# Where a recurrent kernel starts its indirect DMAs inside a step, and where it seeds its PSUM banks

## The reference, cut to what matters

```python
xW = jnp.einsum('ntd,dh->nth', x, Wx) + b          # x: 2 x 1024 x 256

def step(prev_h, xw_t):
    next_h = jnp.tanh(xw_t + prev_h @ Wh)          # Wh: 256 x 256
    return next_h, next_h
_, hs = jax.lax.scan(step, h0, jnp.swapaxes(xW, 0, 1))   # 1024 steps, one after the other

logits = x_flat @ gate_w.T                         # x_flat: the 2048 states, 8 experts
top_v, top_i = jax.lax.top_k(logits, 2)
combine = ...                                      # softmax of the two, by expert and token
hidden = silu(x_flat @ wg[e].T) * (x_flat @ wu[e].T)     # per expert, 256 -> 1024
acc = acc + combine[e][:, None] * (hidden @ wd[e].T)     # 1024 -> 256
return x + acc
```

## Time and profile before

| | us |
|---|---|
| median of 3 runs | 847.75 (846.58 to 849.95) |
| the profiled execution | 847.57 |
| its span in the profile | 845.5 |
| PE busy / ACT busy / DVE busy / POOL busy | 741.6 / 479.4 / 441.4 / 112.0 |
| the tanh (L843), 1024 of them: busy; idle before them, for PE's L474 | 161.9; 300.4 |
| the ring's low part (L1175), 1024: busy; idle before them, for ACT's L843 | 166.1; 339.3 |
| matmuls of the ring (L474, wh_hi): idle before them, for DVE's L1175 | 74.0 |

### The profile page before, as it was taken

One profiled execution on the slowest core, in us unless ns is written; L12 is line 12 of the kernel. 1 busy time (PEld: TensorE's weight loads), 2 busy tenths in 40 slices (PEclk: granted clock), 3 DMA queues, 4 the chain that ended last, 5 costly groups with the idle time before them and its releaser, 6 DMA issues.

```text
span 845.5 us, 41906 instructions
## 1 busy us (share of the span) xinstructions
PE 741.6 (88%) x17106; PEld 645.1 (76%) x17106; DVE 441.4 (52%) x2572; ACT 479.4 (57%) x2839; POOL 112.0 (13%) x104
## 2 busy tenths in 40 slices
PE   6555555699999999999999999999999999998894
PEld 4443444588888888888888888888888888887784
DVE  4776767454454545454544445454545444455542
ACT  4776777555555555555655556555555555554442
POOL 1000000001111101101020111111021101123222
PEclk7555555599999999999999999999999999999997
DMA  4676766501111111111120111111111111111111
GB/s 131 194 198 183 205 186 184 183 10 38 19 35 22 35 22 24 34 20 31 22 41 16 29 23 34 29 26 25 19 39 22 34 16 29 24 17 39 29 29 23
DMA packets 35149, 49.01 MB, mean 58 GB/s; under 512 B 5232, under 2 KB 21616, under 8 KB 34928
## 3 DMA queue, kind: packets, MB, share of 16 engines
q1 hardware_dynamic: 27200, 36.53, 15.7%
q0 software_dynamic: 7488, 9.57, 7.2%
q10 hardware_dynamic: 272, 0.26, 0.1%
HBM read 35.57 MB, written 12.88 MB: 57 GB/s over the span
## 4 chain that ended last, share of the span: by engine, by line
PE 78%; DVE 6%; ACT 6%; DMA 4%; issue 4%; another core or an unknown queue 0%; POOLq 0%; ACTq 0%; SPq 0%; DVEq 0%
PE bank L474 35%; PE bank L597 24%; PE bank L619 12%; DVE state L1175 4%; ACT bank L843 4%; DMA arena<-w_all 3%; PE bank L628 3%; PE bank L456 1%; PE bank L576 1%; DMA out<-y_sb,place_now 1%; PE bank L568 1%; ACT w_hi L829 1%; DVE arena L1103 0%; DMA b_sb<-bias_in 0%
## 5 line engine op out<-in xcount | busy, mean ns | idle before, releaser
L1175 DVE TENSOR_TENSOR state<-bank,state 128x4 f16<-128x4 f32 x1024 | 166.1, 162 | 353.7 <-ACT bank L843 339.3
L474 PE MATMUL bank<-state,wh_hi 128*128 128x4 f16 (+1 forms) x4204 | 264.8, 168 | 83.1 <-DVE state L1175 74.0
L843 ACT ACTIVATE bank<-bank 128x4 f32<-128x4 f32 x1024 | 161.9, 158 | 306.1 <-PE bank L474 300.4
L474 PEld LDWEIGHTS bank<-state,wh_hi 128*128 128x128 f16 x4204 | 176.5, 98 | 172.4 <-DVE state L1175 115.3
L474 PE MATMUL bank<-state,wh_lo 128*128 128x2 f16 x4096 | 245.4, 163 | 0.0
L474 PEld LDWEIGHTS bank<-state,wh_lo 128*128 128x128 f16 x4096 | 177.5, 97 | 0.0
L835 ACT ACTIVATE state<-bank 128x4 f16<-128x4 f32 x1024 | 175.1, 171 | 2.8 <-PE bank L474 2.7
L597 PE MATMUL bank<-x_T,w_hi 128*128 128x128 f16 (+1 forms) x1856 | 154.8, 206 | 4.6 <-issue 2.6
L619 PE MATMUL bank<-arena,w_hi 128*128 128x128 f16 (+1 forms) x1600 | 140.1, 208 | 0.3 <-DVE arena L1110 0.2
L597 PE MATMUL bank<-x_T,w_lo 128*128 128x128 f16 (+1 forms) x928 | 138.1, 206 | 0.0
L597 PE MATMUL bank<-arena,w_hi 128*128 128x128 f16 (+1 forms) x1344 | 129.0, 211 | 1.7 <-issue 1.3
(11 more groups left out here) (141 smaller groups left out, 971.4 us busy)
## 6 DMA issues: line engine op xcount, KB each, us to landing
arena<-w_all SPq DMA_DIRECT2D x96, 256.0 KB
xrow<-expert_rows SPq DMA_DIRECT2D x82, 66.0 KB
early<-xT SPq DMA_DIRECT2D x17, 128.0 KB
expert_rows<-pad SPq DMA_DIRECT2D x8, 132.0 KB, 3.2
expert_rows<-rows,slot POOLq DMA_INDIRECT x34
out<-y_sb,place_wide POOLq DMA_INDIRECT x30
out<-y_sb,place_now POOLq DMA_INDIRECT x20, 3.2
arena<-wh_in ACTq DMA_DIRECT2D x1, 256.0 KB, 4.2
```

The costliest lines, as they stand in the source:

```text
L474: return pe.matmul(out, w[:, k, m * P:(m + 1) * P], moving, start=False, stop=False, skip_group_check=True)
L843: act.activation(h32_at(n), preact(n), ACT.Tanh, scale=1 / SCALE).then_inc(s_h32, 1)
L1175: v.tensor_tensor(lo[:, i, :, B * tt:B * tt + B], h32_at(n).rearrange("p (c b) -> p c b", c=2), hi[:, i, :, B * tt:B * tt + B], ALU.subtra ...
```

## The change

Every indirect DMA of the loop is pinned in one way: a scatter or an add at step n waits for the tanh of step n-1. The adds move from o = 16 to 18, the scatters from o = 0, 6, 12 to 0, 4, 10, all steps that have one of VectorE's long operations. The seeds move from the steps 0, 1, 2 of a block to 3, 4, 5 (the first block keeps its place), and the waits for them move along.

```diff
+SEED_AT = 3
-ADD_AT, SCATTER_AT = (16, 22), (0, 6, 12)
+ADD_AT, SCATTER_AT = (18, 22), (0, 4, 10)
...
     def count_step(blk):
-        return scatter_steps(blk)[0] - 1 if blk == NBLK - 1 else scatter_steps(blk)[1] - 3
+        return scatter_steps(blk)[0] - 1 if blk == NBLK - 1 else scatter_steps(blk)[1] - 2
...
+        def seed_at(blk):
+            return SEED_AT if blk else FIRST
+
         def seeds(n):
             blk, t = divmod(n, STEPS)
-            return blk < NBLK - 1 and t - first(blk) < 3
+            return blk < NBLK - 1 and 0 <= t - seed_at(blk) < 3
...
-                if blk < NBLK - 1 and tt - first(blk) in (1, 2, 3):
-                    act.wait_ge(s_clr, 3 * blk + tt - first(blk) + 3)
+                if blk < NBLK - 1 and tt - seed_at(blk) in (1, 2, 3):
+                    act.wait_ge(s_clr, 3 * blk + tt - seed_at(blk) + 3)
...
             def pin_to(n):
-                p, o = pair_of(n)
-                half, w = divmod(o, HALF_T)
-                chunk = split_of(n // STEPS, n % STEPS)
-                if p >= 0 and w in HI_AT:
-                    pool.wait_ge(s_hhi, 2 * (2 * p + half) + HI_AT.index(w) + 1)
-                elif chunk is not None:
-                    pool.wait_ge(s_ch, chunk + 1)
-                else:
-                    pool.wait_ge(s_h32, n - FIRST)
+                pool.wait_ge(s_h32, n - FIRST + 1)
...
-            def add_half(p, half, weighed, added, s=s_scat):
+            def add_half(p, half, weighed, added, s=s_scat, at=None):
+                if at is not None:
+                    pin_to(at - 1)
...
-            def add_static(p, half):
+            def add_static(p, half, at=None):
                 if not wide(p):
-                    add_half(p, half, parts(p) + half + 1, 16 * parts(p) + 16 * half)
+                    add_half(p, half, parts(p) + half + 1, 16 * parts(p) + 16 * half, at=at)
                 elif half == 0:
+                    if at is not None:
+                        pin_to(at - 1)
                     pool.wait_ge(s_y, parts(p) + 1)
...
-                    add_static(p - 1, ADD_AT.index(o))
+                    add_static(p - 1, ADD_AT.index(o), n)
```

More of the change, by code:

```diff
@@ L1178, in step @@
                 if seeds(n):
-                    v.wait_ge(s_zh, LEAD + 3 * blk + tt - first(blk) + 1)
+                    v.wait_ge(s_zh, LEAD + 3 * blk + tt - seed_at(blk) + 1)
                     v.tensor_copy(xw[(n + 2) % 3][:, (1 - i) * P:(1 - i) * P + SEEDS], seed_cols).then_inc(s_clr, 1)
```

## The result

| | before | after |
|---|---|---|
| median of 11 runs each, on one chip (us) | 848.53 (845.46 to 850.54) | 853.14 (850.75 to 855.84) |
| profiled execution (us) | 847.57 | 855.73 |
| its span (us) | 845.5 | 854.0 |

The change makes the kernel slower: the ratio is 1.0052, with a 95% interval of 1.0036 to 1.0068, 4.6 us by the medians. The two profiled executions lie 8.2 us apart, since that of before is from the lower half of its runs and that of after from the top of its own. Sums made from the two traces are therefore too large by some 3.5 us; what one DMA costs can be read from either.

What follows compares the result with a forecast made beforehand. The kernel was taken as bound by the latency of a 0.70 us ring from tanh to tanh, with ScalarE held after each indirect DMA. 4.0 + 1.7 - 0.6 = +5.1 on 847.57 gave 852.7 us, range 848.5 to 857.5.

Steps and rivals of the forecast that it cites:

- The new place costs 0.43: 58 moved DMAs, each making the second tanh 0.43 us late instead of 0.36: 24.9 us against 20.9, +4.0 us.
- The hold is ScalarE's: After an indirect DMA starts, ScalarE itself starts no instruction between about 0.8 and 1.3 us, though TensorE signalled in time.
- The six early scatters, +1.7: Scatters before 240 us: the second tanh would come 0.35 us late, 2.1 us together instead of 0.4, +1.7 us.
- The end of the loop, -0.6: The last DMAs queue behind one another and slide past the last step, so their cost goes: -0.6 us.
- Seeds: Seeded steps stay 0.06 us longer and the wait moves along: 0, with bounds of 2.7 us either way.
- VectorE's operation: Rival, chance 0.20: the next step's long VectorE operation delays the hold, so the tanh due at 0.97 passes; 838 us.
- The early end of the hold: Rival, chance 0.15: the hold ends at 1.33 us after each start, a DMA costs 0.36 as now; 848.7 us.
- No pair of tanhs 1.4 apart: Sign in the profile after: no tanh caught at the hold's front, so no two tanhs 1.4 us apart any more.

Runs made afterwards that it cites:

- e8_who: Changed kernel with 14 independent ScalarE copies in each wide add's step and 12 VectorE copies in each scatter's; no neighbouring copies began more than 0.10 us apart; no ratio given.
- e9_thick: Changed kernel with TensorE's filler matmuls also in steps n = 84 to 215; five early scatters cost 0.40, 0.43, 0.40, 0.40 and 0.57 us; no ratio given.
- e11_tiny: Changed kernel with eight 8-column matmuls in each step n = 84 to 215; five early scatters cost 0.41, 0.43, 0.44, 0.42 and 0.58 us; no ratio given.
- e4_seeds: Only the seeds move, against the kernel before; the DMAs stay at their old places; ratio to before 0.999 (0.9977 to 1.0003).
- e3_nolong: Changed kernel with adds at o = 20, scatters at 2 and 8, no long VectorE operation in the next step; second tanh 0.50 and 0.44 us late in the mean.
- e10_gap: Changed kernel with early fillers, but TensorE's matmuls thinned in three steps round each scatter; 18 of 22 wide-pair scatters cost 0.01 us at most; no ratio given.
- e7_delay: Changed kernel with a 128x240 POOL memset before each scatter or wide add of the wide pairs; ratio to before 1.0012 (0.9997 to 1.0028).

## Why the prediction was right, and where it was not

The forecast was 852.7 and the median is 853.14; as a change, +5.1 was forecast and +4.6 measured. The main term holds, two others do not, and that the total still came out is in part luck, as said at the end.

*The new place costs 0.43.* Right: what exceeds 0.70 in the two steps behind each of the 51 starts from n = 240 to 975 is 22.6 us, where I had 21.9, and 15.8 before, where I had 15.3. The first of the two tanhs was never caught there.

*The hold is ScalarE's.* Wrong. I wrote that TensorE had its signal in time and ScalarE starts nothing; e8_who shows ScalarE starting something every 0.10 us. What comes late is TensorE's result or signal, 0.39 to 0.76 after the end of the ring's last matmul. The empty stretch of ScalarE was there because every instruction of ScalarE in it stood behind a tanh that waited. The number came out right, since the tanh shows the end of the hold whoever is held.

*The six early scatters, +1.7.* This step failed: -0.3 in the traces (0.46 us before in the two steps behind each start, 0.18 after). I carried the main loop's hold into steps in which TensorE has 715 matmuls in 60 us and not its full load; with 1027 or 1378 (e9_thick, e11_tiny) the loss was there. The earlier trace rows showed a tanh held at 1.20; at 1.0 there was no row.

*The end of the loop, -0.6.* Wrong. From n = 1045 to the end the profiled loop takes 9.83 us, before 9.34: +0.5. The DMAs did slide, but onto each other, and a hold of two in a row cost 1.86. With the narrow pairs' 0.5 for each DMA, the loop from n = 976 on gave back 0.7 instead of 3.2.

*Seeds.* Right: e4_seeds is at 0.999. In the changed kernel's eighth block the steps from 323.10 to 325.38 are 0.76 each, 0.06 longer as before.

*The rivals.* VectorE's operation neither breaks nor makes the hold (e3_nolong, e9_thick). The Trainium skill (SBUF — State Buffer, Who interferes with whom) has VectorE and GpSimd contend and no other engine. e8_who agrees on ScalarE; on TensorE the tanh 0.49 late differs, and the measurement decides, though whether a port of SBUF is the cause no run shows. The early end of the hold is out, since 0.43 is above its 0.36. No pair of tanhs 1.4 apart was forecast: one of 1.44 is left in the wide pairs, behind the scatter at 528.78, one of 1.56 in the narrow pairs, at 754.29, where the first tanh is caught, and the 2.56 above. The forecast's own range, 848.5 to 857.5, does not follow from its terms: 0.36 and 0.50 a DMA give 848.7 and 856.8.

The failed terms nearly cancel, which is luck: 2.0 too much at the early scatters, 2.5 too little at the end. The steps without a DMA from n = 240 to 975 lose 9.0 us in the profile after, 6.9 before; in the other kernels' profiles it is anything between, so I put it down to the execution and not to the change. The base helped as well: the forecast stands on the profiled 847.57, 1.0 below the median of the eleven runs.

## What to carry to other kernels

An indirect DMA of POOL in a tight ring through TensorE costs time by where it starts and by TensorE's load round it, that before its start included. With a lighter load TensorE's results are held later and the ring's can get through (18 scatters in e10_gap); with one long matmul in place of eight short ones the early scatters cost 0.02 instead of 0.4. Before an idle stretch is laid to an engine, fill it with work that waits for nobody: one run told ScalarE from TensorE. A hold found in one stage is not carried to another in which the load of the engine behind it is different.

## What was not expected of the hardware

TensorE's result is held while the DMA engines do next to nothing. The DMA view of the changed kernel from 294.1 to 295.7 us, in which a scatter starts at 294.21 and a tanh comes 0.43 late at 295.61:

```profile
DMA packets 0, 0.00 MB, mean 0 GB/s; under 512 B 0, under 2 KB 0, under 8 KB 0
```

Behind 46 of the 51 DMAs at most two packets move in the first 1.4 us. So it is neither the transfer nor a packet of any other queue. What is left is something that POOL's instruction does before its data move; no run shows what. TensorE itself goes on meanwhile: behind most of the 51, matmuls start up to 1.25 after the DMA's start. The Trainium skill (DMA: Bandwidth & Descriptors, SWDGE vs HWDGE vs iDMA) has GpSimd write descriptors into rings in SBUF before an engine moves a byte; the empty window agrees, and no run here shows the rings. What this does to TensorE, and why its load moves the front of the hold and not its end, stays open. Also, POOL's wait for a semaphore that POOL itself raises took 0.43 us (e7_delay).
